# A two-layer attention and experts kernel: later parts for two query batches, four gathers ahead, and a reordered last sum

## The reference, cut to what matters

```python
x = x + _L0_xattn_ref(_layernorm(x), ctx_768, ...)   # one head of 128
x = x + _L0_ffn_ref(_layernorm(x), ...)              # 64 experts, 6 per token, 64 slots each
x = x + _L1_xattn_ref(_layernorm(x), ctx_768, ...)   # 16 heads of 8
x = x + _L1_ffn_ref(_layernorm(x), ...)              # 8 experts, 2 per token, at most 160 tokens per choice
```

```python
q = x @ Wq.T + bq                                     # third step
attn = softmax(einsum('bihd,bjhd->bhij', q, k) * SCALE)
out = einsum('bhij,bjhd->bihd', attn, v) @ Wo.T + bo
...
keep = (cumsum(onehot, axis=0) <= capacity) * onehot  # fourth step
w = einsum('tk,tke->te', topv, keep)
h = gelu(einsum('td,edf->etf', xt, W1) + b1)
y = einsum('etf,efd->etd', h, W2) + b2
out = einsum('te,etd->td', w, y)
```

## Time and profile before

| | us |
|---|---|
| time, median of 3 runs | 318.76 (317.25 to 319.27) |
| profiled execution, its own time | 317.57 |
| its span, first to last instruction | 315.4 |
| PE busy | 269.7 (86%) |
| DVE busy | 200.7 (64%) |
| ACT busy | 140.3 (44%) |
| POOL busy | 119.1 (38%) |

### The profile page before, as it was taken

How to read it: one execution, slowest core, us unless ns; L and a number is a source line. 1 busy time by engine, 2 the same in 40 slices (tenths; PEclk the granted TensorE clock), 3 DMA queues, 4 the chain that set the end, 5 groups by cost and what they waited for, 6 DMA issues and landing times.

```text
span 315.4 us, 5674 instructions
## 1 busy us (share of the span) xinstructions
PE 269.7 (86%) x2046; PEld 171.1 (54%) x2046; DVE 200.7 (64%) x633; ACT 140.3 (44%) x273; POOL 119.1 (38%) x152
## 2 busy tenths in 40 slices
PE   0997867699999999866699999998999999997783
PEld 0656623357888877642134455534545457775661
DVE  2566698838888555484988778746365866653235
ACT  1454341016555566332338767686637323343121
POOL 5867154787554430025011111120010173787710
PEclk9999597855999999995559999999999999999798
DMA  7953658148888899546325530019310010111152
GB/s 196 305 143 144 171 136 165 17 41 45 182 175 176 175 186 188 117 84 176 93 68 160 114 71 2 4 57 333 97 35 0 2 42 21 44 43 42 50 145 67
DMA packets 22911, 34.01 MB, mean 108 GB/s; under 512 B 3388, under 2 KB 14804, under 8 KB 22565
## 3 DMA queue, kind: packets, MB, share of 16 engines
q1 hardware_dynamic: 19523, 28.48, 33.4%
q0 software_dynamic: 2080, 4.07, 11.0%
q10 hardware_dynamic: 1282, 1.12, 1.4%
HBM read 23.56 MB, written 7.80 MB: 99 GB/s over the span
## 4 chain that ended last, share of the span: by engine, by line
PE 59%; DVE 15%; issue 11%; POOL 5%; DMA 5%; ACT 4%; ACTq 0%; DVEq 0%; POOLq 0%
PE bank L917 53%; DVE score L1901 3%; DMA packc<-in_packc 2%; POOL expert_rows L665 2%; POOL xg L612 1%; DMA big<-q_parts 1%; PE bank L1247 1%; DVE xn L1498 1%; PE bank L1111 1%; POOL splits L656 1%; POOL rstd L562 1%; DMA q_parts<-parts 1%; DMA splits<-normalised,sslot 1%; PE bank L1370 1%; POOL xg L656 1%
## 5 line engine op out<-in xcount | busy, mean ns | idle before, releaser
L1901 DVE TENSOR_REDUCE score<-bank 128x2 f32<-128x512 f32 x64 | 41.9, 686 | 13.1 <-PE bank L917 12.3
L612 POOL DMA_INDIRECT xg<-normalised,slot_token x32 | 37.4, 1168 | 25.0 <-PE bank L1063 12.1
L863 ACT ACTIVATE pbuf<-bank 128x512 f32<-128x512 f32 x64 | 37.1, 598 | 15.5 <-PE bank L917 15.1
L917 PE MATMUL bank<-ks,big 128*128 128x256 bf16 x128 | 29.1, 319 | 5.3 <-DVE score L1901 3.7
L562 POOL TENSOR_TENSOR rstd<-veps,mhalf 128x4 f32<-128x4 f32 (+1 forms) x10 | 9.0, 899 | 61.9 <-DVE veps L1490 59.7
L917 PE MATMUL bank<-big,ks 128*128 128x256 bf16 x128 | 24.8, 281 | 0.4 <-ACT pbuf L863 0.4
L917 PEld LDWEIGHTS bank<-ks,big 128*128 128x128 bf16 x128 | 9.6, 104 | 24.3 <-DVE score L1901 13.8
L627 POOL CAST nmp<-score 128x16 bf16<-128x16 f32 x8 | 1.6, 196 | 49.1 <-DVE score L1901 49.1
L1620 DVE TENSOR_TENSOR pbuf<-rk,iota_s 128x4096 bf16<-128x4096 bf16 (+1 forms) x10 | 18.5, 1855 | 2.1 <-DMA xg<-normalised,slot_token 2.0
L917 PE MATMUL bank<-pbuf,vaug 128*9 128x256 f32 x256 | 19.7, 381 | 0.0
L656 POOL DMA_INDIRECT xg<-normalised,sslot x12 | 11.5, 962 | 21.4 <-DVE sslot L1834 18.0
(11 more groups left out here) (240 smaller groups left out, 581.6 us busy)
## 6 DMA issues: line engine op xcount, KB each, us to landing
big<-in_w SPq DMA_DIRECT2D x8, 704.0 KB, 7.6
big<-in_w SPq DMA_DIRECT2D x8, 384.0 KB, 9.4
big<-in_ew SPq DMA_DIRECT2D x12, 256.0 KB, 5.5
ks<-k_parts SPq DMA_DIRECT2D x2, 1024.0 KB, 10.3
big<-ks SPq DMA_DIRECT2D x8, 256.0 KB, 4.9
big<-q_parts SPq DMA_DIRECT2D x8, 256.0 KB, 4.0
k_parts<-parts SPq DMA_DIRECT2D x2, 768.0 KB, 4.6
q_parts<-parts SPq DMA_DIRECT2D x8, 192.0 KB, 2.4
```

Source lines behind the costliest of these rows:

```text
L612: pool.indirect_dma_start(out=xg[:, g % 2, j, :], out_offset=None, in_=xn_dram, in_offset=bass.IndirectOffsetOnAxis(ap=slot_token[:, g % N ...
L863: a.activation(prob1[:, e % NPROB, :], bank[2 + e % 2][:, :], ACT.Exp).then_inc(a_exp, 1)
L917: return pe.matmul(out_, lhsT, rhs, start=start, stop=stop, skip_group_check=True)
L1901: v.tensor_reduce(nm1[:, c, 2 * hp:2 * hp + 2], bank[m % 2][:, :].rearrange("p (h k) -> p h k", h=2), X, ALU.max, negate=True).then_inc(a_ ...
```

## The change

Five things move, and two small operations are exchanged.

1. The queries of batches 2 and 3 are scaled by ACT (an Identity activation with a scale and a bias, L819 of the new kernel) in place of DVE, ahead of the loop. A new DVE instruction of one column makes the scaled bias first.
2. Their second and third parts move from slots 0 to 3 to slots 16 to 18 (batch 2) and 21 to 23 (batch 3), on DVE and ACT.
3. SP sends the queries of batch 2 after the maxima of group 1, and those of batch 3 after the maxima of group 2.
4. `AHEAD` becomes 4. The numbers of expert 3 are made in the last slot of the loop, its gather is issued ahead of scatter 0, and `sparse_outputs(i)` stands ahead of `sparse_numbers(i + 4)` on PE. On DVE the one-hots of `i + 4` come first in iteration `i`, its addresses last, and `last_tokens` moves from `i` = 3 to `i` = 2.
5. At the end DVE adds both planes to both halves first, and then the two last sums.

```diff
+QUERY_REST = {17: 2, 22: 3}
...
-NUMBERS_STEP = {76: 0, 77: 1, 78: 2}
-VALUES_AT = {76: 0, 77: 1, 78: 2}
-AHEAD = 3
+NUMBERS_STEP = {76: 0, 77: 1, 78: 2, 81: 3}
+VALUES_AT = {76: 0, 77: 1, 78: 2, 81: 3}
+AHEAD = 4
...
                 maxima_stacked(k)
-                if k < 2:
-                    queries_stacked(2 + k)
+                if 1 <= k < 3:
+                    queries_stacked(1 + k)
...
+            def scaled_queries(b):
+                a.wait_ge(q1_f, b)
+                a.wait_ge(q1_ps, b + 1)
+                a.activation(qf[:, batch(b)], bank[6 + b % 2][:, 0:TB], ACT.Identity,
+                             bias=bias_q1[:, 0:1], scale=SCALE1).then_inc(q1_f, 1)
...
-            query_parts(2)
-            query_parts(3)
+            for b in (2, 3):
+                scaled_queries(b)
+                query_first(b)
...
             for s in range(SLOTS):
                 m, e = s, s - LAG
+                if s in QUERY_REST:
+                    query_second(QUERY_REST[s])
...
                 if i + 1 < ES:
                     sparse_transposes(i + 1)
+                sparse_outputs(i)
                 if i + AHEAD < ES:
                     sparse_numbers(i + AHEAD)
-                sparse_outputs(i)
...
+            def query_bias():
+                v.wait_ge(ld_small, 64)
+                v.tensor_scalar(bias_q1[:, :], biases[:, B_BQ1:B_BQ1 + 1], SCALE1, None, ALU.mult)
...
-                for i, step in enumerate((queries, query_residual, query_last)):
-                    if s in (i, i + 1):
-                        step(2 + s - i)
+                if s + 1 in QUERY_REST:
+                    query_residual(QUERY_REST[s + 1])
+                if s - 1 in QUERY_REST:
+                    query_last(QUERY_REST[s - 1])
...
             for i in range(ES):
+                if i + AHEAD < ES:
+                    sparse_onehots(i + AHEAD, 0)
+                    sparse_onehots(i + AHEAD, 1)
                 sparse_bias(i)
+                sparse_weighted(i)
                 if i + AHEAD < ES:
                     sparse_values(i + AHEAD)
-                sparse_weighted(i)
-                if i + AHEAD + 1 < ES:
-                    sparse_onehots(i + AHEAD + 1, 0)
-                    sparse_onehots(i + AHEAD + 1, 1)
-                if i == AHEAD:
+                if i == ES - AHEAD:
                     last_tokens()
...
+            for h2 in range(2):
+                cs = slice(4 * h2, 4 * h2 + 4)
                 v.wait_ge(f_oT, len(LAST_CHUNKS) + h2 + 1)
```

More of the change, by code:

```diff
@@ L133, in build @@
         mhalf = sb("mhalf", [P, 4])
+        bias_q1 = sb("bias_q1", [P, 1])
         zero = sb("zero", [P, 1])
@@ L813, in _, with query_first, query_second @@
                        ).then_inc(z_sb, 1)
-            def query_parts(b):
+            def scaled_queries(b):
[3 more added lines that the diff above has]
+                             bias=bias_q1[:, 0:1], scale=SCALE1).then_inc(q1_f, 1)
+            def query_first(b):
                 a.wait_ge(q1_f, b + 1)
                 a.copy(parts[:, 0, batch(b)], qf[:, batch(b)]).then_inc(q1_hi, 1)
+            def query_second(b):
                 a.wait_ge(q1_res, b + 1)
@@ L825, in _ @@
             norm_transposed(5)
-            query_parts(0)
+            query_first(0)
+            query_second(0)
             a.wait_ge(z_T, 3)
             norm_transposed(6)
-            query_parts(1)
+            query_first(1)
+            query_second(1)
             a.wait_ge(z_T, 4)
             norm_transposed(7)
-            query_parts(2)
-            query_parts(3)
+            for b in (2, 3):
+                scaled_queries(b)
+                query_first(b)
             a.wait_ge(ln_tsb, 8)
@@ L1348, in sparse_numbers @@
             def sparse_numbers(i):
-                pe.wait_ge(s_oh, AHEAD + i + 1 if i < AHEAD else 2 * (i + 1))
+                pe.wait_ge(s_oh, 3 + i + 1 if i < 3 else 2 * (i + 1))
                 if i >= 1:
@@ L1731, in _ @@
             statistics2(2)
+            query_bias()
             queries(0)
```

## The result

| | before | after |
|---|---|---|
| median of 7 runs each, us | 318.49 (316.99 to 320.31) | 314.40 (312.61 to 319.32) |
| after to before, ratio with 95% interval | | 0.9874 (0.9828 to 0.9921) |
| profiled execution, its own time | 317.57 | 312.61 |
| its span | 315.4 | 310.4 |
| PE, DVE, ACT, POOL busy | 269.7, 200.7, 140.3, 119.1 | 268.5, 200.6, 140.9, 119.1 |

The account below looks back on a forecast made before the run. DVE's row maxima were taken to pace the early loop, gather waits the sparse experts, DVE the last sums. Gains of 0.5 - 0.1 + 4.2 + 0.6 = 5.2 us gave a median of 313.0, range 311.6 to 314.9.

Parts of the forecast that it names:

- Sparse experts: From the loop's end to expert 5's outputs: four gathers ahead remove PE's gather waits, gain 4.2 us (3.0 to 4.7).
- Last sums: End of the kernel: DVE's reordered sums take 0.9 us less, of which 0.6 was taken (0.2 to 0.9).
- The return of the scattered rows: Near the end: returned rows arrive some 1 us ahead of their use, so hidden, barely.
- The new column on DVE: Ahead of the loop: the new one-column instruction delays batch 0's load by 0 to 0.23 us, 0.1 taken.
- First exponential: Near slot 17: the table load stands uncovered behind a cast, so it starts at 163.5 against 163.88, 0.35 us gained.
- The loop: Attention loop, slots 0 to 48: moving the queries of batches 2 and 3 gains 0.5 us (-1.0 to 1.4).
- The sum of 5.2: Whole kernel: 0.5 (loop) - 0.1 (new column) + 4.2 (sparse experts) + 0.6 (last sums) = 5.2 us less.
- The clock came back in time: Rival, attention loop: PE's clock rises late behind a wait, slower than before, 322.5 us if at 185; chance 0.04.
- The fourth gather: Rival, sparse experts: late addresses keep it out of POOL's idle time, experts run as before, 317.3 us; chance 0.03.
- the exponentials come late: Rival, attention loop: table load, casts and a later clock cost 1.0 us instead of gaining 0.5, 314.5; chance 0.15.
- POOL as the bound of the end: Rival, sparse experts and end: stretched POOL transfers bring returned rows 1 to 2 us late, 314.5; chance 0.12.
- the longer switch of tables: Rival, attention loop: extra time behind ACT's table load delays the first exponential by 1.28 us, 314.3; chance 0.03.

Follow-up runs that it names:

- e1: Kernel before with only the change's sparse-expert and last-sum parts, queries as before; median 313.35 us, ratio to before 0.9824.
- e7: Changed kernel with the old order of the last sums, each half's planes and last sum before the next; median 315.43 us, ratio to before 0.9898.
- e3: Changed kernel with batch 3's query hand-off on SP moved behind the maxima of group 3; median 312.28 us, ratio to before 0.9809.
- e6: Changed kernel with only the two zero writes to the planes moved two groups of maxima later; median 312.42 us, ratio to before 0.9801.
- e4: Changed kernel with a one-column exponential on ACT ahead of the loop, so the table loads early; median 313.57 us, ratio to before 0.9822.
- e2: Kernel before with only the change's attention-loop part (queries of batches 2 and 3), old experts and last sums; median 317.44 us, ratio to before 0.9985.
- e8: Changed kernel with PE's old order, numbers of expert i + 4 ahead of outputs of expert i; median 319.24 us, ratio to before 1.0029.
- e5: Changed kernel with both batch 3's hand-off behind group 3's maxima and the early table load; median 311.46 us, ratio to before 0.9797.

## Why the prediction was right, and the step of it that failed

- **Sparse experts, right, by its steps.** Hidden layer 1 starts 8.57 after layer 0 (8.4 taken), the outputs of expert 5 at 297.74 (298.0). What went away is more than 4.18: the waits for gathers 4 and 5 (1.67 and 2.21), and 1.54 of clock, since the outputs of expert 4 ran behind the second wait in the low clock of the earlier trace rows and took 4.61, now 3.07. The rest was given back, as foreseen, by hidden layer 1 starting later and by the 0.2 that PE waits for gelus in each iteration now.
- **Last sums, right in both parts.** 0.57 of 0.6. From the outputs of expert 5 to the end of the last sum DVE took 0.91 less, as worked out; what went was a wait of 0.94 for PE in the middle of the sums (ahead of 309.95 before). From there to the end of the span it is 3.05, before 2.71 (3.07 in e1, and 2.76 in e7 with the old order), about the 0.3 that was allowed for the two halves leaving together. The return of the scattered rows was hidden, barely: in after nothing waits, but with the same tail the third plane sum waits 0.17 for it in e1 and 0.22 in e3.
- **The new column on DVE.** 0.15 busy, between the bounds of 0 and 0.23.
- **First exponential, right.** 14.7 after slot 0 was worked out (163.5 - 148.82), 14.61 measured, and the cause is the one named: the load stands behind the cast. The Trainium skill ("ScalarE: Activation LUTs", What ACT_TABLE_LOAD costs) has a drain of 1.38 us for every switch. The trace disagrees again: the cast ahead of the load ends at 161.41 and the load starts at 161.43; the load ends at 162.71 and the exponential starts at 162.72. That the median came out at the 314.4 which this drain would have given is a coincidence.
- **The loop, failed.** The step was this: "Batch 3 follows eight slots later and is needed 16 later." That is true of batch 3's data, and the wait that came is not one for these. What it left out is what stands behind batch 3 on SP's in-order list: a zero write, which the account of SP's order ahead of the prediction does not name, and the maxima of group 3, wanted in slot 41. Without that wait the later queries are worth 1.1 (100.02 to 98.89 in e3, 98.87 in e6), more than the 0.5 that I took and inside the ends of -1.0 and 1.4. With it, 1.1 - 1.54 = -0.4.
- **What the median holds.** The sum of 5.2 was to give 313.0, the median is 314.4. The failed term is 1.0 of the difference, and 0.3 is the start: the sum went out from 318.2 for before (317.6 + 0.6), and the seven runs have 318.49. What is left is less than the runs can tell. The range is right with some luck: it took 0.35 as the worst of the loop, and -0.46 lies below that; the other terms came out where they were taken, not at their low ends, and left room. And -0.46 is itself no fixed number: with SP's order of after, PE's wait was 0.98, 1.54, 1.91, 2.26 and 2.54. It grew, by and large, with batch 3's hand-off, which took 4.45, 4.86, 4.79, 5.35 and 5.38 in the same executions (e4, after, e2, e7, e8). That the wait also sets the spread of the runs is argued and not shown.
- **The rivals.** The clock came back in time: 0.75 from 164 to 166 and 1.00 behind it. POOL had one transfer stretched to 2.13, beside DVE's `last_tokens` (283.00 to 285.06), as in the earlier trace rows, with 5.1 to spare. The Trainium skill ("SBUF — State Buffer", The DVE blocks DMA trap) agrees with this row, but its price was nothing here. When a transfer is stretched the rows leave open: before, a scatter at 275.54 took 2.07 beside the one-hots of expert 5 (275.45 to 277.22), a second case that the earlier trace rows do not show, and in after a scatter at 270.79 beside the same one-hots (270.49 to 272.31) took 1.06. The fourth gather got into the idle time (262.55 to 265.97). Three rivals lie within 0.1 of the median in their times, and none has the mechanism: "the exponentials come late" (314.5), but the first came 0.45 earlier than before; POOL as the bound of the end (314.5), but no sum waits for it in after; and the longer switch of tables (314.3), but no such time shows.

**Open.** Why batch 3's hand-off takes 4.5 to 5.4 in after, e2, e4, e6, e7 and e8 and 3.0 in e3 and e5 (and 3.0 for batch 2 in after). In the long cases it begins 3.3 to 3.6 after batch 2's stacked load was issued, and such loads took 3.5 to 4.4 to land in after. That alone is not the cause: before, it begins 3.57 after that load (164.56 to 168.13) and takes 3.29.

## What to carry to other kernels

When a transfer moves later in an in-order queue, check what stands behind it as carefully as the data that it carries: the wait that comes may be for a neighbour's few kilobytes. Put a table load where the engine idles anyway, by one small activation, before other work is queued ahead of it. Between two steps of an engine, the one that is ready should stand ahead of the one that waits for somebody, above all on TensorE, where a wait may be paid a second time in clock.

## What was not expected of the hardware

- **A wait of PE that costs almost twice its length.** Behind PE's waits of 0.98, 1.54 and 1.91 in the loop, and one of 1.67 in the sparse experts of before, the next matmuls ran at their usual speed. Behind 2.05, 2.21, 2.26 and 2.54 the clock fell, and 1.5 to 1.6 more were lost. In e7 the level rose again at 192, when PE had been busy without a gap since 188. The length of a wait does not decide it by itself: early in after (42.62) the clock was at 0.50 behind a wait of 1.51, where PE had been busy for only 1.10 of the 2.60 us from 40.00.
- **Small issues beside a large write.** Three issues for the 4 KB maxima rows took 3.4 to 3.7 where the 512 KB of zeros went out just ahead of them (after, e2, e4, e7, e8), 2.4 where these had gone 4.0 to 4.1 earlier (before, e1), and 2.0 to 2.05 where they had gone 4.6 earlier or went later (e3, e5, e6).
